# Value products of a head pair as one block, with the row sums, ahead of the third maxima, scores and projection

## The chip, the cores and the metric

The kernel runs on one core of a Trainium2 chip. The metric is the device time of one launch in microseconds. A core has five engines that run at the same time, each with its own instruction stream in a fixed order: TensorE (PE, matrix products; its weight loads are shown apart as PEld), VectorE (DVE), ScalarE (ACT), GpSimd (POOL) and SyncE (SP, which issues transfers). They wait for one another with semaphores only. Matrix products are written to PSUM, eight banks of 128 partitions by 512 floats; operands lie in SBUF.

## What the kernel computes

Two gated layers on tokens `x` (4 batches of 256 tokens, 128 channels) with a context `ctx` (4 batches of 512). The change is in the attention of the second layer: the tokens are latents that ask, context and latents together (768 keys) are the keys and values, 16 heads of 64 channels:

```
q = lat @ Wq
kv = concat([x, lat], axis=1) @ Wkv
k, v = split(kv)
dots = einsum('bhid,bhjd->bhij', q, k) * scale
attn = softmax(dots, axis=-1)
out = einsum('bhij,bhjd->bhid', attn, v)
return out.reshape(b, m, heads * dim_head) @ Wout
```

Around it, in order: an attention with 16 heads of 8 channels, a feed-forward layer with routed low-rank experts, this attention, and a feed-forward layer with one expert of eight per token. Every step adds its gated output to `x`.

## The kernel before, in words

The whole kernel is written by hand as one stream of instructions per engine, with the semaphore waits written out; no planner moves anything. The order in the Python text of an engine's block is the order in which that engine runs.

The second attention works on head pairs: 4 batches of 8 pairs, 32 pairs `g`, with `p = g % 8` the pair's place in its batch. One turn of the loop at L2235 (called turn `g` here) mixes the work of several pairs on TensorE:

- `max1(g+1, 0)`, `max1(g+1, 1)`, `max1(g+1, 2)` (L2027): the scores of the next pair, laid with queries on the partitions, only to find their row maxima. All three write banks 4 and 5, so each waits until VectorE has reduced the one before (`row_max1`, L1337: reductions at L1343 for parts 0 and 1 and at L1346 for part 2, then a small maximum at L1352 that makes `max_cols`).
- `max_row_in(g+1)` (L2050): turns those maxima into a row. It waits for L1352. ScalarE copies the row out, and `scores1(g+1, 0)` waits for that copy.
- `scores1(g, 0)`, `(g, 1)`, `(g, 2)` (L2056): the scores of pair `g` with keys on the partitions, less the maxima. ScalarE takes the exponential of each third (`exp1`, L813).
- `project(g+3, 0)` and `project(g+3, 1)` (L1993): keys and queries of a pair three ahead, into bank 7. ScalarE copies each half out rounded (`kqh`, L572), VectorE subtracts to get the rest (`proj_low`, L1331, `kql`, L1334), and that frees bank 7.
- `values1(g-1, chunks)` (L2079): values times probabilities of the pair before, six chunks of 128 keys, into the left half of bank 6. `sums1(g-1)` (L2097): the row sums, into the right half of bank 6, from `fold1`, which GpSimd has folded from the probabilities (two additions, L551 and L554, and a fold, L559).
- at the end of a turn `values_in` (into bank 5) and a third use of bank 7: a value projection, the turned context or latents of the next batch (`context_turn`, `latents_turn`, for `p` = 3 and 4), or the output projection of the batch before (`outputs1`, for `p` = 1). The third use waits until bank 7 is free, that is for `kql` of `project(g+3, 1)`.

VectorE runs a turn in this order (L1557 to L1583):

```
row_max1(g + 1, 0)
...
row_max1(g + 1, 1)
proj_low(g + 3, 0)
...
first_slot(g)
row_max1(g + 1, 2)
second_slot(g)
proj_low(g + 3, 1)
...
divide1(g - 1)
```

`divide1` (L1355: a reciprocal at L1359 and a product at L1360) waits for `sums1` and reads bank 6. The slots hold the normalising of the next batch's tokens for `p` = 3 (`context_norm`, L1296, in the first, `latents_norm`, L1285, in the second), steps of the layer norm for some other turns, and for `p` = 4 and 5 a copy `kv_t` (L1306, L1322) stands between `row_max1(g + 1, 0)` and `row_max1(g + 1, 1)`.

Of the kernel before, what the change touches and what calls it, by code (L numbers as in the profile page):

```python
# [47 lines left out]
def flamingo(nc, t_in, out):  # L48
# [24 lines left out]
    G1 = B * NPAIR  # L73
# [4 lines left out]
    with ExitStack() as ctx:  # L78
# [152 lines left out]
        def bank(i, n=1):  # L231
            return ps[:, i * BANK:(i + n) * BANK]
# [146 lines left out]
        def values_of(b, half):  # L379

            m = max(M_AT[u] for u in M_USES if u[:2] == (b, half)) + 1
            x = max(VX_AT[u] for u in VX_AT if u[1:3] == (b, half)) + 1
            return m, x
# [1241 lines left out]
        def _(pe):  # L1625
            def mm(o, lhsT, rhs, start=True, stop=True):
                return pe.matmul(o, lhsT, rhs, start=start, stop=stop)  # L1627
# [399 lines left out]
            def max1(g, part):  # L2027
                s = g % KS
                if part == 0:
                    pe.wait_ge(d_kql.sem, d_kql.after(g, 2))  # L2030
                    if g >= 1:
                        pe.wait_ge(d_max1.sem, d_max1.after(g - 1, 4))
                        pe.wait_ge(a_mrow.sem, g)
                    m = sum(1 for use in M_USES if M_PAIR[use] <= g - 2)
                    if m:
                        pe.wait_ge(a_vM.sem, m)
                else:
                    pe.wait_ge(d_max1.sem, d_max1.after(g, part))
                q = kqh[:, s, NK:NK + NQ]
                if part < 2:  # L2040
                    for j in range(2):
                        ins = mm(bank(4 + j), q[half_of[j], part * P:(part + 1) * P], kqh[half_of[j], s, 0:NC_])
                else:
                    for t in range(TQ):
                        for j in range(2):
                            ins = mm(bank(4 + j)[:, t * NQ:(t + 1) * NQ], q[half_of[j], t * P:(t + 1) * P],
                                     kqh[half_of[j], s, NC_:NK])
                ins.then_inc(e_max1.sem, 1)

            def max_row_in(g):  # L2050
                pe.wait_ge(d_max1.sem, d_max1.after(g, 4))
                for t in range(TQ):
                    ins = mm(tok(bank(4), t), max_cols[:, g % 2, t, :], negidentb[:, :])
                ins.then_inc(e_mrow.sem, 1)

            def scores1(g, u):  # L2056
                n = 3 * g + u
                s = g % KS
                if u == 0:
                    pe.wait_ge(a_mrow.sem, g + 1)  # L2060
                if n == 1:
                    pe.wait_ge(d_kql.sem, d_kql.after(2, 2))
                if n >= 2:
                    pe.wait_ge(a_exp1.sem, n - 1)
                q_h, q_l = kqh[:, s, NK:NK + NQ], kql[:, s, NK:NK + NQ]
                for k in (2 * u, 2 * u + 1):
                    o = [bank(2 * (n % 2) + j)[:, (k % 2) * NQ:(k % 2 + 1) * NQ] for j in range(2)]
                    at = slice(k * P, (k + 1) * P)
                    for j in range(2):
                        mm(o[j], kqh[half_of[j], s, at], q_h[half_of[j], :], True, False)  # L2070
                    for j in range(2):
                        mm(o[j], kql[half_of[j], s, at], q_h[half_of[j], :], False, False)
                    for j in range(2):
                        mm(o[j], kqh[half_of[j], s, at], q_l[half_of[j], :], False, False)
                    for j in range(2):
                        ins = mm(o[j], onesb[half_of[j], :], max_row[half_of[j], g % 2, :], False, True)
                ins.then_inc(e_st1.sem, 1)

            def values1(g, chunks):  # L2079
                b, p = divmod(g, NPAIR)  # L2080
                if chunks[0] == 0:
                    if g >= 1:
                        pe.wait_ge(d_o1.sem, g)
                    if p % 4 == 0:
                        m, x = values_of(b, p // 4)
                        pe.wait_ge(a_vM.sem, m)
                        pe.wait_ge(a_vX.sem, x)
                pe.wait_ge(a_exp1.sem, a_exp1.after(g, chunks[-1] // 2 + 1))
                for k in chunks:
                    for j in range(2):  # L2090
                        h = 2 * p + j
                        ins = mm(bank(6)[j * D1:(j + 1) * D1, 0:NQ], v1[:, k, h * D1:(h + 1) * D1],
                                 p1[:, g % 2, k // 2, j * BANK + (k % 2) * NQ:j * BANK + (k % 2 + 1) * NQ],
                                 k == 0, k == TK - 1)
                ins.then_inc(e_pv1.sem, 1)

            def sums1(g):  # L2097
                pe.wait_ge(g_fold.sem, g + 1)
                for j in range(2):
                    ins = mm(bank(6)[j * D1:(j + 1) * D1, NQ:2 * NQ], onesf[:, :], fold1[:, g % 2, j, :])  # L2100
                ins.then_inc(e_den1.sem, 1)
# [55 lines left out]
            def turned_in1(i):  # L2157
                pe.wait_ge(d_xnD.sem, i + 1)
                if i == 0:
                    pe.wait_ge(d_kql.sem, d_kql.after(G1, 0))  # L2160
                if i == 1:
                    pe.wait_ge(d_o1.sem, G1)
                if i >= 2:
                    pe.wait_ge(a_mT.sem, i)
                transpose_tiles(bank(HEAD_BANK[i]), xnD[:, i % 2, :, :], TQ).then_inc(e_xTD.sem, 1)

            def head1(i):
                pe.wait_ge(a_xTD.sem, i + 1)
                mm(bank(HEAD_BANK[i])[0:E, NQ:2 * NQ], gate1[:, :], xTD[:, i % 2, :]).then_inc(e_lgD.sem, 1)

            def probs1(i):
                pe.wait_ge(d_prob.sem, i + 1)
                if i >= 1:
                    pe.wait_ge(a_b2.sem, i)
                transpose_tiles(bank(7), probT[:, :].rearrange("p (t d) -> p t d", t=TQ), TQ).then_inc(e_pT.sem, 1)

            def masks1(i):
                pe.wait_ge(d_mask.sem, i + 1)
                transpose_tiles(bank(HEAD_BANK[i]), maskp[:, i % 2, :, :], TQ).then_inc(e_mT.sem, 1)
# [55 lines left out]
            for g in range(G1 + 1):  # L2235
                b, p = divmod(g, NPAIR)
                if g < G1:
                    if g + 1 < G1:
                        max1(g + 1, 0)
                    scores1(g, 0)  # L2240
                    if g == G1 - 3:
                        turned_in1(0)
                    if g == G1 - 2:
                        probs1(0)
                    scores1(g, 1)
                    if g + 1 < G1:
                        max1(g + 1, 1)
                    if g + 3 < G1:
                        project(g + 3, 0)
                    if g == G1 - 3:  # L2250
                        head1(0)
                    if g == G1 - 1:
                        masks1(0)
                        wide_masks1(0, 0)
                if g == G1:
                    wide_masks1(0, 1)
                    bias1(0)
                if g >= 1:
                    values1(g - 1, (0, 1, 2, 3))
                if g < G1:  # L2260
                    if g + 1 < G1:
                        max1(g + 1, 2)
                    scores1(g, 2)
                    if g + 3 < G1:
                        project(g + 3, 1)
                if g >= 1:
                    values1(g - 1, (4, 5))
                    sums1(g - 1)
                if g < G1:
                    if g + 1 < G1:  # L2270
                        max_row_in(g + 1)
                    if values_use(g) is not None:
                        values_in(*values_use(g))
                    use = third_use(g)
                    if use is not None:
                        if use[0] == "v":
                            values_in(*use[1:])
                        elif use[0] == "ctx":
                            context_turn(use[1])
                        elif use[0] == "lat":  # L2280
                            latents_turn(use[1])
                        else:
                            outputs1(use[1])
# [52 lines left out]
```

## Time and profile before

| what | us |
|---|---|
| median of 3 runs | 828.2 (823.18 to 828.38) |
| the profiled execution | 827.83 |
| its span, first to last instruction | 826.0 |
| PE busy | 740.4 (90%) |
| DVE busy | 574.0 (69%) |
| ACT busy | 360.6 (44%) |
| POOL busy | 282.4 (34%) |

The profiled execution takes 1.8 us more than its span, and 0.4 us less than the median. A row of a timeline gives the start and the duration of an instruction (or of several of one kind that follow each other, with their count), its engine, line, operation, output and inputs, and in brackets how long the engine stood idle before it and whose instruction ended that. TensorE runs each product of 32-bit floats in two passes, so the count of its rows is twice the number of products in the text.

### The profile page before, as it was taken

How to read it: one execution, taken by the hardware profiler on the slowest of the kernel's cores; microseconds unless marked ns; L12 is line 12 of the kernel's file. 1: busy time of each engine (PE TensorE's matmuls, PEld its weight loads, DVE VectorE, ACT ScalarE, POOL GpSimd, SP SyncE). 2: the span in 40 equal slices, each digit the busy share in tenths (PEclk: the TensorE clock that was granted, in tenths of full speed). 3: DMA queues.
4: the chain of work that ended last, by engine and by line, in shares of the span. 5: the costliest groups of instructions: out<-in, count | busy, mean ns of one | idle time of the engine just before them, and what ended most of it. 6: DMA issues, size and time to landing. Idle time of an engine off the chain costs nothing.

```text
span 826.0 us, 14271 instructions
## 1 busy us (share of the span) xinstructions
PE 740.4 (90%) x5654; PEld 549.9 (67%) x5654; DVE 574.0 (69%) x1100; ACT 360.6 (44%) x533; POOL 282.4 (34%) x203
## 2 busy tenths in 40 slices
PE   6779989996987997889999899989999787999996
PEld 5656556654776875656777677766677555887894
DVE  4767777654778686897667876587767876577543
ACT  2666665762343435345444445444444333320300
POOL 4265444410100102454554455445554453100000
PEclk9789999997999998999999999999999998999998
DMA  8000000005000021000000000000000000000000
GB/s 175 9 1 2 2 1 2 2 2 204 2 1 0 1 70 34 1 1 2 1 2 1 2 1 2 1 1 2 1 2 2 1 1 1 1 8 1 7 7 6
DMA packets 25552, 11.55 MB, mean 14 GB/s; under 512 B 11832, under 2 KB 24200, under 8 KB 25360
## 3 DMA queue, kind: packets, MB, share of 16 engines
q1 hardware_dynamic: 24480, 10.59, 5.0%
q8 instruction: 45, 0.74, 0.4%
q10 hardware_dynamic: 1008, 0.07, 0.1%
q14 instruction: 19, 0.16, 0.1%
HBM read 10.06 MB, written 0.52 MB: 13 GB/s over the span
## 4 chain that ended last, share of the span: by engine, by line
PE 71%; DVE 20%; issue 4%; ACT 3%; DMA 1%; SPq 0%; DVEq 0%; ACTq 0%
PE ps L1627 68%; PE ps L1638 2%; DVE mx L1068 2%; DVE o L1359 2%; ACT v L572 1%; DVE max_cols L1352 1%; DVE pmax L1343 1%; DVE pmax L1346 1%; DVE xnC L1285 1%; DVE kql L1334 1%; DVE ysum L1494 1%; DVE cn L1296 1%; ACT kqh L572 1%; PE ps L1731 1%; DMA raw<-in_L_xattn_Wproj_dram 1%
## 5 line engine op out<-in xcount | busy, mean ns | idle before, releaser
L813 ACT ACTIVATE p<-ps 128x1024 f32<-128x1024 f32 x96 | 96.7, 1025 | 146.1 <-PE ps L1627 146.1
L1627 PE MATMUL ps<-p,v 128*64 128x256 f32 (+1 forms) x1280 | 131.9, 389 | 4.1 <-DVE xr L1091 2.0
L551 POOL TENSOR_TENSOR acc<-p 128x1024 f32<-128x1024 f32 x32 | 76.0, 2374 | 154.7 <-ACT p L813 154.7
L1627 PE MATMUL ps<-kqh 64*128 64x256 f32 (+1 forms) x640 | 109.9, 379 | 11.9 <-ACT v L572 4.3
L1068 DVE TENSOR_REDUCE mx<-ps 128x1 bf16<-128x512 f32 x128 | 82.5, 687 | 34.7 <-PE ps L1627 33.9
L1343 DVE TENSOR_REDUCE pmax<-ps 128x2 f32<-128x1024 f32 x64 | 78.2, 1222 | 38.4 <-PE ps L1627 37.2
L554 POOL TENSOR_TENSOR acc<-acc,p 128x1024 f32<-128x1024 f32 x32 | 76.0, 2375 | 69.7 <-ACT p L813 69.7
L1627 PEld LDWEIGHTS ps<-p,v 128*64 128x64 f32 (+1 forms) x1280 | 64.0, 126 | 53.1 <-issue 18.9
L1627 PEld LDWEIGHTS ps<-kqh 64*128 64x128 f32 x640 | 62.0, 202 | 37.6 <-issue 29.5
L524 POOL TENSOR_SCALAR q<-qst,rmask 128x256 fp32r<-128x256 f32 x64 | 58.9, 938 | 65.3 <-ACT qst L572 65.3
L668 ACT ACTIVATE p<-ps 128x1024 f32<-128x1024 f32 x64 | 65.4, 1025 | 27.8 <-PE ps L1627 25.8
L1334 DVE TENSOR_TENSOR kql<-ps,kqh 128x512 fp32r<-128x512 f32 x64 | 44.1, 691 | 34.2 <-ACT kqh L572 33.9
L1359 DVE RECIPROCAL o<-ps 128x256 f32<-128x256 f32 x32 | 56.2, 1755 | 6.2 <-PE ps L1627 3.6
L1627 PE MATMUL ps<-max_row,onesb 64*128 64x256 bf16 x384 | 59.8, 293 | 0.0
L1627 PE MATMUL ps<-kqh,kql 64*128 64x256 f32 x384 | 59.5, 292 | 0.0
L1627 PE MATMUL ps<-kql,kqh 64*128 64x256 f32 x384 | 58.8, 288 | 0.0
L1627 PE MATMUL ps<-kst,q 128*128 128x512 f32 x128 | 49.1, 435 | 4.6 <-DVE mx L1068 4.2
L1346 DVE TENSOR_REDUCE pmax<-ps 128x4 f32<-128x1024 f32 x32 | 39.1, 1220 | 18.9 <-PE ps L1627 18.8
L1627 PE MATMUL ps<-q,kst 128*128 128x256 f32 x256 | 46.7, 304 | 0.4 <-ACT p L668 0.4
L1627 PEld LDWEIGHTS ps<-q,kst 128*128 128x128 f32 x256 | 34.5, 189 | 13.5 <-issue 7.0
L572 ACT ACTIVATE kqh<-ps 128x512 fp32r<-128x512 f32 x64 | 38.0, 594 | 11.0 <-PE ps L1627 8.5
L1627 PEld LDWEIGHTS ps<-kqh,kql 64*128 64x128 f32 x384 | 41.9, 201 | 0.5
(282 smaller groups left out, 1561.8 us busy)
## 6 DMA issues: line engine op xcount, KB each, us to landing
w<-in_L_ffn_W_dram SPq DMA_DIRECT2D x1, 2048.0 KB, 12.0
wt<-in_L_ffn_W_dram SPq DMA_DIRECT2D x4, 512.0 KB, 6.1
ctx_all<-in_ctx_dram SPq DMA_DIRECT2D x4, 256.0 KB, 5.4
raw_kv<-in_L_xattn_Wkv_dram SPq DMA_DIRECT2D x1, 1024.0 KB, 4.9
raw<-in_L_ffn_B_dram SPq DMA_DIRECT2D x9, 64.0 KB
xr<-in_x_dram SPq DMA_DIRECT2D x4, 128.0 KB, 3.9
raw_q<-in_L_xattn_Wq_dram SPq DMA_DIRECT2D x1, 512.0 KB, 5.8
wout<-in_L_xattn_Wout_dram SPq DMA_DIRECT2D x1, 512.0 KB, 7.1
```

Source lines behind the costliest of these rows:

```text
L524: pool.tensor_scalar(q4[:, q % SLOTS, v, :], qst[:, q % 2, :], rmask[:, v:v + 1], None, ALU.mult).then_inc(g_q4.sem, 1)
L551: pool.tensor_tensor(acc1[:, :], p1[:, s, 0, :], p1[:, s, 1, :], ALU.add).then_inc(g_acc.sem, 1)
L554: pool.tensor_tensor(acc1[:, :], acc1[:, :], p1[:, s, 2, :], ALU.add).then_inc(g_acc.sem, 1)
L572: return act.activation(to, of, ACT.Copy)
L668: act.activation(p0[:, n % PR0, :], bank(2 * (n % 2), 2), ACT.Exp).then_inc(a_exp0.sem, 1)
L813: act.activation(p1[:, g % 2, u, :], bank(2 * (n % 2), 2), ACT.Exp, scale=SCALE1).then_inc(a_exp1.sem, 1)
L1068: dve.tensor_reduce(mx0[:, q % 2, n % 2, n // 2:n // 2 + 1], bank(4 + m % 2), AX, ALU.max).then_inc(d_max0.sem, 1)
L1334: dve.tensor_tensor(kql[:, g % KS, at], bank(X_BANK.get(("proj", g, half), 7)), kqh[:, g % KS, at], ALU.subtract).then_inc(d_kql.sem, 1)
L1343: dve.tensor_reduce(pmax[:, g % 2, 0, part, :], m.rearrange("p (j k) -> p j k", j=2), AX, ALU.max).then_inc(d_max1.sem, 1)
L1346: dve.tensor_reduce(pmax[:, g % 2, 1, :, :].rearrange("p t j -> p j t"), m.rearrange("p (j t k) -> p j t k", j=2, t=TQ), AX, ALU.max).then ...
L1359: then(dve.reciprocal(o1[:, g % OS, :], bank(6)[:, NQ:2 * NQ]))
L1627: return pe.matmul(o, lhsT, rhs, start=start, stop=stop)
```

## The change

In the loop over pairs on TensorE the second part of the value products and the row sums move up: they come straight behind the first four chunks, ahead of `max1(g+1, 2)`, `scores1(g, 2)` and `project(g+3, 1)`. No instruction is added or removed, no wait changes, and the streams of the other engines stay as they are.

```
                 if g >= 1:
                     values1(g - 1, (0, 1, 2, 3))
+                    values1(g - 1, (4, 5))
+                    sums1(g - 1)
                 if g < G1:
                     if g + 1 < G1:
                         max1(g + 1, 2)
                     scores1(g, 2)
                     if g + 3 < G1:
                         project(g + 3, 1)
-                if g >= 1:
-                    values1(g - 1, (4, 5))
-                    sums1(g - 1)
-                if g < G1:
                     if g + 1 < G1:
                         max_row_in(g + 1)
```

## Rows read from the trace of the kernel before

**Rows 1.** The page: busy time by engine, and the chain of waits by engine.
```profile
PE 740.4 (90%) x5654; PEld 549.9 (67%) x5654; DVE 574.0 (69%) x1100; ACT 360.6 (44%) x533; POOL 282.4 (34%) x203
...
PE 71%; DVE 20%; issue 4%; ACT 3%; DMA 1%; SPq 0%; DVEq 0%; ACTq 0%
```

**Rows 2.** Timeline of PE, turn 17: start us, duration us, what.
```profile
516.62 0.50 PE L1627 MATMUL ps<-kqh 64*128 64x512 f32 x2
...
519.83 0.63 PE L1627 MATMUL ps<-kqh 64*128 64x256 f32 x6
...
522.13 1.08 PE L1627 MATMUL ps<-p,v 128*64 128x256 f32 x8
...
523.58 0.28 PE L1627 MATMUL ps<-negidentb,max_cols 128*128 128x128 bf16 x2
...
524.44 3.73 PE L1627 MATMUL ps<-wout,o 128*128 128x128 f32 x32
...
530.28 0.48 PE L1627 MATMUL ps<-kqh 64*128 64x512 f32 x2
```

**Rows 3.** Timeline of DVE, turns 13, 14, 16 and 17.
```profile
473.85 1.23 DVE L1343 TENSOR_REDUCE pmax<-ps 128x2 f32<-128x1024 f32 x1 [0.47 <-PE ps L1627]
...
484.81 1.23 DVE L1343 TENSOR_REDUCE pmax<-ps 128x2 f32<-128x1024 f32 x1 [0.92 <-PE ps L1627]
...
506.71 1.23 DVE L1343 TENSOR_REDUCE pmax<-ps 128x2 f32<-128x1024 f32 x1 [0.92 <-PE ps L1627]
...
515.36 1.21 DVE L1343 TENSOR_REDUCE pmax<-ps 128x2 f32<-128x1024 f32 x1
517.17 1.23 DVE L1343 TENSOR_REDUCE pmax<-ps 128x2 f32<-128x1024 f32 x1 [0.60 <-PE ps L1627]
...
521.63 0.18 DVE L1352 TENSOR_TENSOR max_cols<-pmax 128x4 bf16<-128x4 f32 x1
522.87 0.69 DVE L1334 TENSOR_TENSOR kql<-ps,kqh 128x512 fp32r<-128x512 f32 x1 [1.06 <-ACT kqh L572]
```

**Rows 4.** Timeline of DVE, turns 3 and 5 (one row each), 11 and 12.
```profile
355.75 1.23 DVE L1343 TENSOR_REDUCE pmax<-ps 128x2 f32<-128x1024 f32 x1 [0.93 <-PE ps L1627]
...
380.45 1.22 DVE L1343 TENSOR_REDUCE pmax<-ps 128x2 f32<-128x1024 f32 x1 [0.47 <-PE ps L1627]
...
448.36 1.22 DVE L1343 TENSOR_REDUCE pmax<-ps 128x2 f32<-128x1024 f32 x1 [0.92 <-PE ps L1627]
...
452.37 1.21 DVE L1346 TENSOR_REDUCE pmax<-ps 128x4 f32<-128x1024 f32 x1
...
453.69 3.74 DVE L1285 TENSOR_SCALAR xnC<-xr,token_moments,rt_y 128x128 f32<-128x128 f32 x2
457.36 0.68 DVE L1334 TENSOR_TENSOR kql<-ps,kqh 128x512 fp32r<-128x512 f32 x1
457.96 1.74 DVE L1359 RECIPROCAL o<-ps 128x256 f32<-128x256 f32 x1
...
460.08 1.21 DVE L1343 TENSOR_REDUCE pmax<-ps 128x2 f32<-128x1024 f32 x1
461.21 0.80 DVE L1306 TENSOR_SCALAR kv_t<-ps,lncols 128x512 f32<-128x512 f32 x1
```

**Rows 5.** Timeline of POOL: the second addition in turns 11 and 28.
```profile
453.63 2.38 POOL L554 TENSOR_TENSOR acc<-acc,p 128x1024 f32<-128x1024 f32 x1 [2.03 <-ACT p L813]
...
656.42 2.37 POOL L554 TENSOR_TENSOR acc<-acc,p 128x1024 f32<-128x1024 f32 x1 [5.77 <-ACT p L813]
```

**Rows 6.** Timeline of DVE: normalising in turn 28, a divide in turn 31.
```profile
655.66 0.60 DVE L1285 TENSOR_SCALAR xnD<-xr,token_moments,rt_y 128x128 f32<-128x128 f32 x2
...
692.59 1.76 DVE L1359 RECIPROCAL o<-ps 128x256 f32<-128x256 f32 x1 [3.57 <-PE ps L1627]
```

**Rows 7.** Timeline of PE: the turned context at the end of turn 11.
```profile
458.09 0.66 PE L1638 MATMUL ps<-ident,cn 128*128 128x128 f32 x4 [2.30 <-DVE kql L1334]
```

**Rows 8.** Stretch behind that wait: busy us of each engine, then TensorE's granted clock.
```profile
458.10:462.50 4.40, 4.40 (x40) 3.47 (x40) 3.87 (x4) 1.31 (x2) 0.00 (x0) 0.68 0.02 6
```

More of the change, by code:

```diff
@@ L2259, in _ @@
                     values1(g - 1, (0, 1, 2, 3))
+                    values1(g - 1, (4, 5))
+                    sums1(g - 1)
                 if g < G1:
@@ L2265, in _ @@
                         project(g + 3, 1)
[L2266 to L2269, printed above, removed]
                     if g + 1 < G1:
```

## The prediction, on record before the run

> **What bounds the kernel now.** I read the page first: TensorE is busy 90% of the span and holds 71% of the chain of waits, VectorE 20% [rows 1]. So most of the time is TensorE's, and a change of its order pays only where it stands idle. Then I took the timelines of the second attention, engine by engine, for turns of every kind, because shares over the span don't tell what a turn waits for.
>
> A plain turn (one from `max1(g+1,1)` to the next) lasts 10.96 us: the reductions of that part start at 473.85 and 484.81 [rows 3]. TensorE fills it nearly whole. But VectorE is close behind: in turn 17 the reduction of `max1(g+1,0)` runs from 515.36, with no idle time before it, since the divide before it has only just ended, and `max1(g+1,1)` starts on TensorE at 516.62, right when that reduction is done [rows 2, 3]. That is the point to watch: VectorE's queue has the divide between the last `kql` of a turn and the first reduction of the next, and TensorE can't go past `max1(g+1,1)` without that reduction.
>
> Turns with `p` = 3 are different. There the reduction of part 2 comes late, at 452.37, behind the normalising of the context; the two `latents_norm` operations then take 3.74 us, while GpSimd's second addition runs from 453.63 for 2.38 us; `kql` waits behind them until 457.36 and the context's turn on TensorE stands idle 2.30 us for it [rows 4, 5, 7]. Behind that gap the mean granted clock is 0.68 for 4.4 us [rows 8], a mixture of 2.4 and 1.2 GHz.
>
> **The change part by part.** Nothing is added, removed or made to wait anew; no DMA and no instruction of SP, ACT, DVE or POOL moves in its own queue. What moves on TensorE is four products and two row sums: from 522.13 to the next instruction at 523.58, 1.45 us [rows 2].
>
> *Inputs of the moved block.* The probabilities and the fold of pair g-1 are done in turn g-1, and `divide1(g-2)`, which frees bank 6, ends before `max1(g+1,1)`. I cost waits of the block itself at nothing; what covers it is a whole turn.
>
> *What stands behind the block now.* Part 2 of the maxima, the last third of scores and `project(g+3,1)` come 1.45 us later. The row of maxima has its `max_cols` ready 1.98 us behind the start of part 2 (519.83 to 521.63 plus 0.18), and the scores and projection take 2.30 us (519.83 to 522.13) [rows 2, 3]: it still costs nothing, but the slack falls from 1.8 us to 0.3.
>
> *The loop through VectorE.* This is the main cost. The divide no longer waits for the sums but for its place in the queue, behind `kql` of the later projection. Round the loop, for a plain turn: `max1(g+1,1)` to part 2 took 3.21 us (516.62 to 519.83), now with the block 4.66; to the projection's end 2.30; ScalarE's copy until `kql` starts 0.74 (522.13 to 522.87); `kql` to the reciprocal 0.60 (457.36 to 457.96, the turn in which nothing stood between them); reciprocal and product until the next reduction 2.12 (457.96 to 460.08); that reduction until `max1(g+1,1)` of the next turn 1.26 (515.36 to 516.62) [rows 2 to 4]. The sum is 11.68 us, above TensorE's 10.96. So a plain turn grows by 0.72.
>
> Would VectorE take the divide early, since its sums are there? In turn 31 it stood idle 3.57 us in front of a reciprocal [rows 6], although a subtraction for the last layer's weights (L1547), whose input ScalarE had long made, stood further back in its queue. So it doesn't pass a waiting instruction, and I charge the loop in full. The Trainium skill, "TensorE: Matmul & The Clock Gate", section "Architectural detail: the array is 16× 32×32, not 1× 128×128", says the same against this change: VectorE's queue is strictly first in, first out. By that rule the sum is about 838; an engine that took whichever was ready would give about 820, as in the first rival.
>
> By kinds of turn:
> - 13 plain turns (`p` = 2 four times; 5, 6 and 7 three times each): 13 x 0.72 = +9.4.
> - `p` = 0, three turns: they last 10.46 (506.71 to 517.17 [rows 3]), as only one use of the banks ends them. They too become 11.68: 3 x 1.22 = +3.7.
> - `p` = 1 with the output projection, three turns: 13.66 now (516.62 to 530.28). Bank 7 comes free only when `kql` ends, 0.74 + 0.69 behind the projection, and 0.05 later the next product starts (458.04 to 458.09) [rows 3, 4, 7]; from the output projection on it takes 5.84 (524.44 to 530.28 [rows 2]). 4.66 + 2.30 + 1.48 + 5.84 = 14.28: 3 x 0.62 = +1.9.
> - `p` = 3 with the turn behind it, three pairs: 24.70 once (355.75 to 380.45) and 25.49 in the other two (448.36 to 473.85) [rows 3, 4]. Here the delay helps. In turn 11 the reduction of part 2 started with no idle time in front of it: VectorE came straight from normalising the context, and 1.26 us later the addition began (452.37 to 453.63). Now the scores come 1.45 us later and the addition, which follows their exponential, with them, while the context's normalising stays where it is; the queue runs dry and the reduction starts on time. Turn 28 shows what is then left: both normalising operations took 0.60 us, to 656.26, and the addition began at 656.42 [rows 4 to 6]. I take it that they get through. Then the pair costs 2 x 11.68, plus 0.2 because `kv_t` ends 0.67 us behind `max1(g+1,1)` (461.21 + 0.80 against 460.08 + 1.26 [rows 4]) and holds the next projection: 23.56. Change: -1.14 and twice -1.93, -5.0.
> - Turns 1 and 27 have steps of a layer norm in the slots; between nothing and 0.7 each, half taken: +0.8. Turns 28 to 30: TensorE or the last gating chain holds them; nothing taken, 0.7 each as the upper end and as much below.
> - Turn 31: the divide that waited 3.57 us [rows 6] gets its sums ahead of a third of scores, about half of the 2.30: -1.1, which reaches the end, since the last pair waits for that divide.
>
> For how the normalising meets GpSimd the Trainium skill, "SBUF — State Buffer", section "Who interferes with whom", says that the two share a port pair and whoever issues first holds it for its whole instruction. Rows 4 to 6 agree (3.74 us against 0.60), and by that rule a margin of 0.16 us decides the -5.0.
>
> Sum: 9.4 + 3.7 + 1.9 - 5.0 + 0.8 - 1.1 = +9.7. The profiled execution took 827.83, so 837.5; the median of the runs is 0.4 higher, and I predict **838 us**. Ends: 0.15 us of error in the loop over 22 turns is 3, turns 1 and 27 to 30 give 3 either way; with them 832 to 844.
>
> **The rivals.**
>
> *VectorE's loop doesn't bind (not slower).* Place: the divide in front of the first reduction. If the loop is under 10.96, that is if my pieces of 11.68 overlap by 0.72 us more than in the rows they come from, plain turns and `p` = 0 stay as they are, and the turns at `p` = 3 and 4 shrink to 2 x 11: -2.7 and twice -3.5. With +1.9, +0.8 and -1.1 that is -8.1: **820**. For it: the sum is made of rows from different turns, and a change of tile shapes less on TensorE may save a little. Against: every piece is an order in a queue, and turn 17 shows the loop closing already.
>
> *The normalising doesn't get through.* If GpSimd's addition still comes first, each of the three pairs only shifts by 1.45: +4.4 instead of -5.0, **847**. For it: the margin of 0.16 us. Against: turn 28.
>
> *The clock falls.* In turns `p` = 0 and 1 TensorE now stands idle up to 1.4 us in front of the third use of bank 7. The gap of 2.30 us was followed by a clock of 0.68 over 4.4 us [rows 7, 8], which costs 4.4 x 0.32 = 1.4 us. In all six turns it would be +8: **846**; if plain turns fell too, more. Against: those six gaps are shorter than that one.
>
> That the change doesn't do what it says is no rival: TensorE runs the text's order.
>
> **How the numbers follow.** My forecast 0.60, VectorE's loop not binding 0.12, normalising blocked 0.16, clock 0.12. About 1% (8.3 us) is what a measurement of this kernel can tell from no change, so slower begins at 836.5, in the upper two thirds of the forecast's own range: 0.41, with the two slow rivals 0.69. The first rival lies on the lower bound, 819.9: 0.07 faster and 0.05 within; with 0.19 of the forecast the middle has 0.24. The range takes in the forecast, the two slow rivals and the upper part of what lies between forecast and first rival: 829 to 849.
>
> **What would show it.** Right: in plain turns the reciprocal starts at the end of `kql` with no idle time, the reductions of `max1(g+1,1)` follow each other by about 11.7 us, and TensorE waits at `max1(g+1,1)` for a reduction; at `p` = 3 the two `xnC` take 0.6 us and the wait of the turned context falls to about 0.5. Wrong: turns of 10.96 (first rival), `xnC` of several us (second), or rows of 1.2 GHz behind the third use (third).

## The result, and the profile after

The changed kernel takes 843.05 us (median of four runs, 836.16 to 845.33) against 828.29 for the kernel before (four runs, 823.18 to 829.79): a ratio of 1.0175, 95% interval 1.010 to 1.025. It is slower, as forecast, and inside the range; the forecast was 5 us short. The profiled execution took 841.65 us, its span is 839.8, 13.8 more than before.

The page of the kernel after, busy time by engine and the chain by engine, answers to [rows 1]:

```profile
PE 739.4 (88%) x5654; PEld 545.3 (65%) x5654; DVE 559.7 (67%) x1100; ACT 357.3 (43%) x533; POOL 283.9 (34%) x203
...
PE 68%; DVE 20%; issue 7%; ACT 4%; DMA 1%; SPq 0%; ACTq 0%; DVEq 0%
```

TensorE does the same work in the same busy time and fills less of a longer span: it is not busy for 100.4 us (839.8 less 739.4), where it was 85.6. So the question is where TensorE waits. The waits of TensorE in the kernel after, from 315 to 712 us (total, number of times, longest):

```profile
PE ps L1627 <- DVE kql L1334: 13.4, 20, 1.3
PE ps L1627 <- DVE pmax L1343: 8.5, 10, 2.8
PE ps L1627 <- DVE maskb L1434: 4.6, 1, 4.6
...
PE ps L1627 <- POOL fold L559: 1.8, 1, 1.8
```

The first line was one wait of 0.7 us before; it now comes 20 times. The last two are single waits at the end of the attention and did not exist before.

**A plain turn.** Timeline of DVE in the kernel after, turn 14, against [rows 3]:

```profile
485.10 1.22 DVE L1343 TENSOR_REDUCE pmax<-ps 128x2 f32<-128x1024 f32 x1 [0.60 <-PE ps L1627]
...
492.11 0.69 DVE L1334 TENSOR_TENSOR kql<-ps,kqh 128x512 fp32r<-128x512 f32 x1 [1.06 <-ACT kqh L572]
492.71 1.75 DVE L1359 RECIPROCAL o<-ps 128x256 f32<-128x256 f32 x1
494.50 0.42 DVE L1360 TENSOR_TENSOR o<-ps,o 128x256 f32<-128x256 f32 x1
494.84 1.21 DVE L1343 TENSOR_REDUCE pmax<-ps 128x2 f32<-128x1024 f32 x1
496.64 1.23 DVE L1343 TENSOR_REDUCE pmax<-ps 128x2 f32<-128x1024 f32 x1 [0.59 <-PE ps L1627]
```

And of PE in the same turn, against [rows 2]:

```profile
484.55 0.50 PE L1627 MATMUL ps<-kqh 64*128 64x512 f32 x2
...
485.89 2.81 PE L1627 MATMUL ps<-p,v 128*64 128x256 f32 x24
488.53 0.60 PE L1627 MATMUL ps<-fold,onesf 128*64 128x256 f32 x4
489.06 0.62 PE L1627 MATMUL ps<-kqh 64*128 64x256 f32 x6
...
491.25 0.28 PE L1627 MATMUL ps<-negidentb,max_cols 128*128 128x128 bf16 x2
...
492.85 0.50 PE L1627 MATMUL ps<-wkv_h,kv_h 128*128 128x512 f32 x1 [0.56 <-DVE kql L1334]
...
495.87 0.28 PE L1627 MATMUL ps<-max_row,onesb 64*128 64x256 bf16 x2
496.11 0.49 PE L1627 MATMUL ps<-kqh 64*128 64x512 f32 x2
```

The end of the same scores and the start of `max1(g+1,1)` in the kernel before, one turn earlier:

```profile
484.23 0.30 PE L1627 MATMUL ps<-max_row,onesb 64*128 64x256 bf16 x2
484.27 0.50 PE L1627 MATMUL ps<-kqh 64*128 64x512 f32 x2
```

Read the two together. The sums of the divide start at 488.53, yet the reciprocal starts only at 492.71, straight behind `kql`: its place in the queue holds it, not its data. Four VectorE operations then run without a gap, and `max1(15,1)` starts on TensorE at 496.11, right behind the reduction (494.84 plus 1.21). TensorE waits about 0.20 us for it, which no bracket shows: 0.24 us lie between the start of the last products of the scores and that of `max1`, where 0.04 lay before. The longer wait of the turn, 0.56 us, is the one for `kql` in front of the third use of bank 7. The turn is 11.54 us (485.10 to 496.64), where it was 10.96.

**The turn with `p` = 3.** DVE of the kernel after, turn 11, against [rows 4]:

```profile
454.63 1.22 DVE L1346 TENSOR_REDUCE pmax<-ps 128x4 f32<-128x1024 f32 x1 [0.63 <-PE ps L1627]
...
455.97 0.60 DVE L1285 TENSOR_SCALAR xnC<-xr,token_moments,rt_y 128x128 f32<-128x128 f32 x2
457.13 0.69 DVE L1334 TENSOR_TENSOR kql<-ps,kqh 128x512 fp32r<-128x512 f32 x1 [0.57 <-ACT kqh L572]
```

The reduction now waits for its scores, the two `xnC` take 0.60 us instead of 3.74, and GpSimd's second addition of this turn begins at 456.69, just behind their end at 456.57.

**By kinds of turn** (us from one reduction of `max1(g+1,1)` to the next):

| turns | before | after | change of one | forecast |
|---|---|---|---|---|
| plain | 10.95 | 11.55 | +0.60 | +0.72 |
| `p` = 0 | 10.46 | 11.55 | +1.09 | +1.22 |
| `p` = 1 | 13.63 | 14.20 | +0.57 | +0.62 |
| `p` = 3 and 4, three pairs | 24.70, 25.49, 25.50 | 23.38, 23.38, 23.37 | -1.32, -2.11, -2.13 | -1.14, -1.93, -1.93 |

From turn 1 to turn 30 the sum is +8.8 us (330.48 to 674.68 before, 328.06 to 681.05 after; forecast +10.8). Ahead of turn 1 the execution after is 2.4 shorter, in code that the change does not touch. The rest (called the tail here), from the reduction in turn 30 to the end, went from 151.32 to 158.75 us: +7.4, where I had -1.1. That is the surprise.

**The end of the attention.** Stretches of the kernel after: from turn 30's reduction to the turned mask products, to the last layer's first products, through the first 16 of these, to the end (busy us of PE, PEld, DVE, ACT, POOL, then the granted clock):

```profile
681.05:696.55 15.50, 9.77 (x84) 6.19 (x85) 12.02 (x20) 4.50 (x6) 9.13 (x4) 0.83 0.01 2
696.55:712.42 15.87, 11.30 (x95) 7.33 (x95) 11.19 (x8) 3.30 (x4) 4.50 (x2) 0.82 0.00 1
712.42:717.95 5.53, 5.53 (x18) 4.51 (x18) 0.00 (x0) 3.64 (x5) 0.00 (x0) 0.62 0.00 0
717.95:839.80 121.85, 110.10 (x675) 95.33 (x673) 69.47 (x130) 21.39 (x37) 6.40 (x4) 0.97 0.02 5
```

The same four of the kernel before:

```profile
674.68:686.69 12.01, 9.41 (x85) 6.71 (x85) 10.60 (x20) 4.35 (x6) 5.99 (x3) 0.78 0.01 1
686.69:700.76 14.07, 10.39 (x96) 6.87 (x94) 8.94 (x8) 4.34 (x6) 5.99 (x3) 0.94 0.01 2
700.76:704.21 3.45, 3.45 (x18) 3.04 (x17) 0.00 (x0) 3.22 (x5) 0.00 (x0) 1.00 0.00 0
704.21:826.00 121.79, 110.03 (x675) 95.33 (x673) 69.42 (x130) 21.81 (x38) 6.41 (x4) 0.98 0.02 5
```

The loss lies in the first three: 3.5 + 1.8 + 2.1 us. `w_l` (L1547) is the subtraction for the last layer's weights, `maskb` (L1434) the masks by which that layer picks its expert. DVE of the kernel after there:

```profile
690.55 2.06 DVE L1547 TENSOR_TENSOR w_l<-wt,w_h 128x1024 fp32r<-128x1024 f32 x1
692.53 3.96 DVE L1434 TENSOR_SCALAR maskb<-iota_ed,topf 128x1024 bf16<-128x1024 bf16 x2
```

POOL of the kernel after:

```profile
689.14 2.39 POOL L554 TENSOR_TENSOR acc<-acc,p 128x1024 f32<-128x1024 f32 x1 [5.81 <-ACT p L813]
691.60 2.13 POOL L559 TENSOR_TENSOR fold<-acc 128x512 f32<-128x512 f32 x1
693.87 2.34 POOL L551 TENSOR_TENSOR acc<-p 128x1024 f32<-128x1024 f32 x1
```

And PE of the kernel after:

```profile
680.93 5.23 PE L1627 MATMUL ps<-p,v 128*64 128x256 f32 x24
...
696.55 1.03 PE L1627 MATMUL ps<-identb,maskb 128*128 128x128 bf16 x8 [4.62 <-DVE maskb L1434]
...
708.66 0.65 PE L1627 MATMUL ps<-fold,onesf 128*64 128x256 f32 x4 [1.80 <-POOL fold L559]
...
712.42 5.69 PE L1627 MATMUL ps<-xm,w 128*128 128x256 f32 x16
```

In the kernel before the same two operations stood at another moment, with GpSimd idle (its fold ended at 682.78, its next addition began at 687.42):

```profile
683.50 1.21 DVE L1547 TENSOR_TENSOR w_l<-wt,w_h 128x1024 fp32r<-128x1024 f32 x1
684.63 0.87 DVE L1434 TENSOR_SCALAR maskb<-iota_ed,topf 128x1024 bf16<-128x1024 bf16 x2
```

After the change the subtraction `w_l` meets the addition (2.06 us instead of 1.21), the fold meets `w_l` (2.13 instead of about 1.28), and the masks meet the fold and the next addition (3.96 instead of 0.87). TensorE waits 4.62 us for the masks. The kernel before had another collision here: `max_cols` of turn 30 met the addition and took 2.02 us, and TensorE waited 2.13 for it. In the kernel after, the block of values of turn 30 (24 rows for twelve products; the rounded products of scores and projections have one row each) takes 5.23 us, for which turn 14 needed 2.81: nearly twice as long, at a granted clock of 0.53, so mostly at the lower of the two clock levels (1.2 GHz of 2.4). The last layer's first 16 products take 5.69 instead of 3.62, at a granted clock of 0.62.

### The profile page after: what moved, and what is told of

It is laid out like the page before. It is cut to its first block, busy times and chain, and to the rows that moved or that the text cites. A ratio compares the mean times of both kernels' runs of the same rounds, so it can differ in the third digit from the quotient of the medians.

```text
span 839.8 us, 14271 instructions
## 1 busy us (share of the span) xinstructions
PE 739.4 (88%) x5654; PEld 545.3 (65%) x5654; DVE 559.7 (67%) x1100; ACT 357.3 (43%) x533; POOL 283.9 (34%) x203
## 2 busy tenths in 40 slices
DMA packets 25552, 11.55 MB, mean 14 GB/s; under 512 B 11832, under 2 KB 24200, under 8 KB 25360
## 4 chain that ended last, share of the span: by engine, by line
PE 68%; DVE 20%; issue 7%; ACT 4%; DMA 1%; SPq 0%; ACTq 0%; DVEq 0%
PE ps L1627 66%; DVE o L1359 2%; ACT kqh L572 2%; DVE kql L1334 2%; DVE mx L1068 2%; PE ps L1638 2%; DVE pmax L1343 1%; DVE w_l L1547 1%; DVE ysum L1494 1%; DVE pmax L1346 1%; DVE rt_t L1262 1%; PE ps L1731 1%; DMA raw<-in_L_xattn_Wproj_dram 1%; DVE rs_t L945 1%; DVE maskb L1434 0%
## 5 line engine op out<-in xcount | busy, mean ns | idle before, releaser
L1627 PE MATMUL ps<-p,v 128*64 128x256 f32 (+1 forms) x1280 | 128.7, 393 | 2.9 <-DVE xr L1091 2.0
L1627 PE MATMUL ps<-kqh 64*128 64x256 f32 (+1 forms) x640 | 104.8, 370 | 13.7 <-DVE pmax L1343 9.1
L1627 PEld LDWEIGHTS ps<-p,v 128*64 128x64 f32 (+1 forms) x1280 | 68.4, 130 | 55.0 <-issue 22.7
L1627 PEld LDWEIGHTS ps<-kqh 64*128 64x128 f32 x640 | 56.2, 192 | 41.0 <-issue 23.4
L1627 PE MATMUL ps<-max_row,onesb 64*128 64x256 bf16 x384 | 55.5, 282 | 0.0
L1627 PE MATMUL ps<-kqh,kql 64*128 64x256 f32 x384 | 55.3, 281 | 0.0
L1627 PE MATMUL ps<-kql,kqh 64*128 64x256 f32 x384 | 54.6, 278 | 0.0
L559 POOL TENSOR_TENSOR fold<-acc 128x512 f32<-128x512 f32 x32 | 42.8, 1336 | 2.5
```

## Experiments

**Theory.** The loss in the turns is the loop through VectorE's queue: `kql`, divide, first reduction, `max1(g+1,1)`, block, part 2, projection, `kql`. What counts is how much work stands between `max1(g+1,1)` and the projection.

**Rivals:** another wait (bank 7, the clock, the block as such) sets the longer turn; GpSimd's additions, met at other moments, are the whole loss. The kernel before, run again beside them, took 825.58 us beside the first four and 823.98 beside the last four; ratios are against these.

**Only the values move.** The row sums stay behind the projection (the edit against the changed kernel):

```
                     values1(g - 1, (4, 5))
-                    sums1(g - 1)
                 ...
                         project(g + 3, 1)
+                if g >= 1:
+                    sums1(g - 1)
```

> Only the two last chunks of the value products move up; the row sums stay in front of the row of maxima. Theory (the loop through VectorE: what is put in front of the later projection delays kql, the divide behind it, the first reduction and so the next max1 part 1): a plain turn falls from the 11.55 us of the changed kernel by the length of the row sums, 0.53 us, to about 11.0. Rival (the block as such costs, by its changes of tile shape on TensorE): a plain turn stays at 11.5 or more, as there is one change of shape more. Device time by the theory: some 12 us under the changed kernel, 827 to 833; by the rival 840 or more.

Measured: 828.01 us, ratio 1.0022 (0.9988 to 1.0056), plain turns 11.11, `p` = 1 turns 13.77, the two `xnC` 0.60 together. In a plain turn of this kernel the trace shows no wait of TensorE for bank 7, the reciprocal still starts straight behind `kql`, and `max1` waits about 0.15 us for its reduction: here it is the loop through the divide that holds the turn. The values are 0.92 of the 1.45 us that the change puts in front of part 2, and cost 0.16 us a turn; the sums, the other 0.53 us, cost a further 0.44. That is what a loop does that had some slack first: 0.76 of the 0.92 us went into it, hardly any of the 0.53.

**The block at `p` = 3 alone.** The new order in turns 3, 11 and 19, the old one elsewhere:

```
+                early = p == 3 and b + 1 < B
                 ...
+                if g >= 1 and early:
+                    values1(g - 1, (4, 5))
+                    sums1(g - 1)
                 ...
-                if g >= 1:
+                if g >= 1 and not early:
                     values1(g - 1, (4, 5))
                     sums1(g - 1)
```

> The new order only in the three turns p = 3 of batches 0 to 2, the old one in all others. Theory: the gain there (the two xnC get through before GpSimd's addition) needs no other turn, and the loss of the plain turns is gone: xnC 0.60 us in place of 3.74 in all three, three pairs of turns shorter by 1.5 to 2.5 us each, plain turns 10.95; 6 us faster than the kernel before, 820 to 824. Rival (the gain at p = 3 comes from the whole loop being slower, so that VectorE has time to spare): xnC still 3.7 us, time as before, 827 to 830.

Measured: 821.77 us, ratio 0.9955 (0.9931 to 0.9978); plain turns 10.95, `p` = 3 turns 11.59 and the turn behind them 11.2, the two `xnC` 0.60. So the change's good part is real and lies in these three turns. The tail of this execution, where nothing differs from the kernel before, took 153.55 us, not 151.32, with a wait of 4.2 us for the masks: the collisions of the tail are not the new order's alone.

**The old order in the last four turns.** The new one for `g` < 28, otherwise the edit of the version above:

```
+                early = g < G1 - 4
```

> The new order in turns 0 to 27, the old one in 28 to 31. Theory: 7 us of the loss arise in the tail, where maskb and w_l of VectorE now run against GpSimd's fold and addition (maskb 3.96 us in place of 0.87, its masks' product waits 4.6 us, and the last layer starts behind the gap at a low clock). With the old order there maskb takes 0.9 us and the time falls by 5 to 7 us against the changed kernel, to 835 to 838. Rival (the tail only inherits a shifted phase from the earlier turns): maskb stays at 2 us or more, time 840 to 844.

Measured: 835.31 us, ratio 1.0105 (1.0067 to 1.0143), the time as expected. The mechanism I gave missed: the masks were blocked here too. DVE of this kernel:

```profile
688.57 2.32 DVE L1547 TENSOR_TENSOR w_l<-wt,w_h 128x1024 fp32r<-128x1024 f32 x1
690.82 2.95 DVE L1434 TENSOR_SCALAR maskb<-iota_ed,topf 128x1024 bf16<-128x1024 bf16 x2
```

From turn 30's reduction to the end it took 153.6 us, against 158.75 with the new order. So the order in the last four turns costs about 5 us against this execution; the remaining 2 of the 7.4 lie between two executions of the old order. Little of the 5 is a longer wait for the masks (4.20 us here, 4.62 there). Its three stretches are 1.9, 1.2 and 2.1 us shorter than those of the kernel after, with granted clocks of 0.88, 0.90 and 1.00 in place of 0.83, 0.82 and 0.62.

**The divide made cheap.** The changed kernel with a copy in place of reciprocal and product:

```
-                then(dve.reciprocal(o1[:, g % OS, :], bank(6)[:, NQ:2 * NQ]))
-                dve.tensor_tensor(o1[:, g % OS, :], bank(6)[:, 0:NQ], o1[:, g % OS, :],
-                                  ALU.mult).then_inc(d_o1.sem, 1)
+                dve.tensor_copy(o1[:, g % OS, :], bank(6)[:, 0:NQ]).then_inc(d_o1.sem, 1)
```

> The changed kernel with the divide left out: instead of reciprocal and product VectorE only copies the value products (about 0.4 us in place of 2.2), so the outputs are not divided by the row sums. Theory: the loop through VectorE falls under 10 us, but bank 7 still comes free only with the later kql, so the third use keeps its 0.5 us of waiting and a plain turn falls only to about 11.45. Rival (the divide is the whole cost): a plain turn falls to the 10.95 of before.

Measured once: 814.18 us, plain turns 11.34, where 11.45 was expected. VectorE now idles in front of the first reduction, and TensorE still waits for bank 7. DVE of this kernel (its lines are two lower from the divide on):

```profile
480.65 0.69 DVE L1334 TENSOR_TENSOR kql<-ps,kqh 128x512 fp32r<-128x512 f32 x1 [1.06 <-ACT kqh L572]
481.26 0.41 DVE L1359 COPY o<-ps 128x256 f32<-128x256 f32 x1
482.83 1.22 DVE L1343 TENSOR_REDUCE pmax<-ps 128x2 f32<-128x1024 f32 x1 [1.16 <-PE ps L1625]
```

And PE:

```profile
481.40 0.50 PE L1625 MATMUL ps<-wkv_h,kv_h 128*128 128x512 f32 x1 [0.54 <-DVE kql L1334]
```

So the divide sets the turn, but only 0.2 us above a second bound: with values and sums gone from behind the projection, too little is left on TensorE to cover `kqh` and `kql` before bank 7 is used again. Without the divide a turn is still 0.39 longer than before, so the shift of work ahead of the projection costs on both paths, and the wait for bank 7 alone would give most of the 0.60. The tail of this kernel, in the new order, took 151.33 us although its masks were held up too (4.00 us): TensorE waited only 2.02 us for them.

**GpSimd's second addition cut, old order, and cut, new order.** In both kernels the addition works on 32 of 1024 columns:

```
-pool.tensor_tensor(acc1[:, :], acc1[:, :], p1[:, s, 2, :], ALU.add).then_inc(g_acc.sem, 1)
+pool.tensor_tensor(acc1[:, 0:32], acc1[:, 0:32], p1[:, s, 2, 0:32], ALU.add).then_inc(g_acc.sem, 1)
```

> The kernel before with GpSimd's second addition (L554) cut to 32 of 1024 columns, so that the row sums lack most of the last third of the keys; all waits stay. Theory: xnC was slow because that addition held the port that VectorE needs, so xnC takes 0.6 us in the old order too, the turned context no longer waits 2.3 us, and the blocked max_cols of turns 0, 1, 27 and 30 (2.1 us) take 0.18; the time falls by 8 to 14 us, to 812 to 818. Rival (xnC is slow by itself or by the late reduction): xnC stays at 3.7 us, time within 3 us of before.

> The same cut in the changed kernel (row sums lack most of the last third). Theory: the gain at p = 3 is then in both kernels and only the loop through VectorE is left of the change: plain turns 11.55 against 10.95; 0.6 us in 13 plain turns and three pairs, 1.1 in three turns p = 0, 0.6 in three turns p = 1, some 17 us in all over the kernel before with the same cut; 829 to 836. The tail's maskb falls to 0.9 us. Rival (the loss is contention with GpSimd as well): the two kernels with the cut are within 5 us.

Measured: old order 805.75 us, ratio 0.9773 (0.9737 to 0.9809), new order 821.40, ratio 0.9955 (0.9926 to 0.9984). The cut by itself gained more than I expected of it, 18 us, so the absolute time of the second missed too; its distance to the first, 15.65 us, is near the 17 expected. What was blocked before is seen in the groups of `max_cols` (shortest, median, longest in ns). The kernel before:

```profile
L1352 DVE TENSOR_TENSOR max_cols<-pmax x32: 175/177/2082, 312.0 to 679.4; 128x4 bf16<-128x4 f32 x32
```

Old order with the addition cut:

```profile
L1352 DVE TENSOR_TENSOR max_cols<-pmax x32: 175/177/180, 310.4 to 659.8; 128x4 bf16<-128x4 f32 x32
```

One expectation missed here: the two `xnC` of the old order took 1.63 us, not 0.60, because GpSimd's fold, now early, runs over them (445.50 to 446.77 against 445.22 to 446.86 in turn 11).

With the addition cut, the new order still makes plain turns of 11.55 and turns 1 to 30 last 348.25 us, 18.5 more than the old (329.74): the loop needs no contention. And the tail is 146.9 in the new order against 147.5 in the old. This sum hides three parts. Up to the last layer's first products the new order is 0.6 us shorter (9.21 + 12.43 against 8.91 + 13.31), where it was 5.3 longer with the addition: that part of the loss needs the addition, and the masks take 0.87 us in both. The first 16 products take 1.7 us longer with the new order here too, so their low clock does not need it. The PE row of the new order with the addition cut, at a granted clock of 0.69 (3.62 us for these products in the old, at 1.00), behind a wait of 2.84 us (2.41 in the old):

```profile
697.80 5.31 PE L1627 MATMUL ps<-xm,w 128*128 128x256 f32 x16
```

The rest of the last layer was 1.7 us shorter in that execution, in code that the change does not touch; its last 43 us had a granted clock of 0.99, where the old order's last 45 had 0.92.

**All six chunks and the sums behind the projection.** A block too, but on the other side:

```
-                if g >= 1:
-                    values1(g - 1, (0, 1, 2, 3))
                 ...
                         project(g + 3, 1)
                 if g >= 1:
+                    values1(g - 1, (0, 1, 2, 3))
                     values1(g - 1, (4, 5))
                     sums1(g - 1)
```

> All six chunks and the sums as one block, but behind maxima part 2, the last scores and the later projection instead of ahead of them. Theory (place, not block): kql is early, the divide waits for the sums and not the other way round; the loop through VectorE is about 10.7 us, and a plain turn is TensorE's own work plus about 0.5 us of waiting for the reduction of part 1 in front of part 2: 11.2 us; at p = 3 xnC is blocked again (3.7 us); 828 to 834 in all. Rival (one block costs wherever it stands): plain turns at 11.5 or more, over 838.

Measured: 826.99 us, ratio 1.0023 (0.9995 to 1.0051), a little below what I expected; plain turns 11.30. The 0.35 that they lose come from the wait that I had expected: part 2 now follows the first projection at once, and TensorE waits for the reduction of part 1 (the divide in turn waits for its sums). PE of this kernel:

```profile
505.83 0.62 PE L1627 MATMUL ps<-kqh 64*128 64x256 f32 x6 [0.42 <-DVE pmax L1343]
```

Part 2 comes early here, and `max_cols` meets the addition in the turns `p` = 3, 4 and 5 (1.08, 1.86 and 1.60 us; the turns last 12.32, 11.28 and 12.28). At `p` = 3 the two `xnC` behind it take 1.56 us, not the 3.7 expected: the addition is over by then, and only the fold runs against them. DVE of this kernel, `p` = 5:

```profile
473.11 1.21 DVE L1346 TENSOR_REDUCE pmax<-ps 128x4 f32<-128x1024 f32 x1
474.35 1.60 DVE L1352 TENSOR_TENSOR max_cols<-pmax 128x4 bf16<-128x4 f32 x1
```

So making one block is not what gives the 11.55; what it costs depends on what it is put in front of.

**The values early at `p` = 3, the sums never.** The two experiments on dose and place point to this version: the two chunks move up in the four turns with `p` = 3, everything else is the old order.

```
+                early = p == 3
                 ...
+                    if early:
+                        values1(g - 1, (4, 5))
                 ...
-                    values1(g - 1, (4, 5))
+                    if not early:
+                        values1(g - 1, (4, 5))
                     sums1(g - 1)
```

> Old order except in the four turns p = 3, where the last two chunks move up but the sums stay. Theory: xnC needs only the 0.9 us of the two chunks to get through, and the sums left behind shorten those turns by another 0.4 us each against the version that moves both: xnC 0.6 us, turns p = 3 of 11.1 us, 819 to 823. Rival (the sums' 0.5 us are needed as well): xnC 3.7 us, 825 to 829.

Measured: 815.05 us, ratio 0.9882 (0.9850 to 0.9913), better than expected and than both kernels. DVE of this kernel, turn 11:

```profile
451.43 0.18 DVE L1352 TENSOR_TENSOR max_cols<-pmax 128x4 bf16<-128x4 f32 x1
451.51 0.60 DVE L1285 TENSOR_SCALAR xnC<-xr,token_moments,rt_y 128x128 f32<-128x128 f32 x2
452.67 0.69 DVE L1334 TENSOR_TENSOR kql<-ps,kqh 128x512 fp32r<-128x512 f32 x1 [0.57 <-ACT kqh L572]
```

0.92 us of delay are enough for `xnC` to get ahead of the addition (452.11 against 452.23), and the sums behind the projection keep cover for bank 7: `p` = 3 turns 11.15, the turn behind them 11.2, plain turns 10.95. The fourth of these turns, 27, gained nothing (14.68, before 14.37).

## Why the prediction was right, and where it was not

*The loop through VectorE: right.* In turn 14 its pieces are 4.51 us to part 2, 2.19 to the projection's end, 0.86 to `kql`, 0.60, 2.13 and 1.27: 11.56 for the 11.68 forecast. The difference is in the first: the six chunks as one group hold TensorE for 2.64 us (485.89 to 488.53), where four and two apart took 1.87 and 0.92 before. That a change of tile shape falls away is my reading; no run tests it. The plain turns thus gave 0.60 instead of 0.72, and `p` = 0 and 1 followed. The rows for it: the reciprocal straight behind `kql`, and the dose in the first experiment. The rival by which the loop does not bind fell with the plain turns of 11.55, in the kernel after and again without the addition.

The Trainium skill, "TensorE: Matmul & The Clock Gate", section "Architectural detail: the array is 16× 32×32, not 1× 128×128", calls VectorE's queue strictly first in, first out. The trace agrees: the sums of turn 14 ended at 489.13 (488.53 plus 0.60), and the reciprocal that reads them started 3.58 us later, when the operations ahead of it in the queue were done.

*A bound that I did not name.* The divide holds the turn only 0.2 us above the third use of bank 7 (11.34 without it). I had written that gaps open there, as a risk to the clock, and not that they are the next limit. On TensorE's side the 0.60 of a plain turn are the 0.56 in front of the third use and the 0.20 in front of `max1(g+1,1)`, less the 0.15 saved in the block. The forecast's loop is the longer of the two paths, but by itself it decides a third of the growth.

*`p` = 3: right.* The scores came later, the normalising did not, and the two `xnC` got through, by 0.12 us where I had read a margin of 0.16. The pairs became 5.6 us shorter, for 5.0 forecast, and the turned context waits 0.55 us in place of 2.30. The rival by which they stay blocked fell with 0.60 us for the two.

*The clock in the turns: right to give it little.* TensorE waits 1.31 us in front of the third use in turn 16 (`p` = 0) and 0.56 in turn 17, and both turns have a granted clock of 1.00.

*Small turns: wrong in sign, small.* Turns 1 and 27 gave -0.4 and -0.6 for the +0.8 taken (half of twice 0.7 would have been 0.7); turn 2 gave 1.2 more than a plain turn, because the lower clock level behind a wait of 2.80 us in turn 1 fell on it (0.90 granted), and turn 29 took 1.2 more than before. Turn 2 was nearly as long with the old order in it (12.53 us where the block moved at `p` = 3 alone), so that part is not the change's.

*Turn 31: the term that failed, inside a sum that held.* By this term the divide gets its sums ahead of a third of scores, and -1.1 reaches the end. The sums did come earlier, and VectorE's idle time in front of that reciprocal fell from 3.57 us [rows 6] to 2.94. But I costed the last turns by the sums alone. `w_l` and the masks stand behind the divide on VectorE; I did not ask which moment they would move to, and it was the one at which GpSimd adds. The runs show +7.4 in the tail in place of -1.1. Four executions with the old order there and the whole addition lie between 150.6 and 153.6 us, so the new order's 158.75 costs 5 to 8; with the values alone moved up it was 156.0. With the addition cut the term has its forecast sign up to the last layer's first products, -0.6. What lowers the clock at these products, and how the rest divides into blocking and clock, stays open, and all these sizes come from single executions.

*The sum: in part luck.* The profiled executions differ by +13.8 where I had +9.7. The turns gave 2.0 less than forecast, the tail 8.5 more, and the 2.4 ahead of turn 1 have nothing to do with the change: these misses partly cancel.

## What to carry to other kernels

Work that moves on one engine moves everything behind it; follow what stands behind it into the queues of the other engines until the path closes on itself, and add up that loop: here TensorE had no more work, and a turn grew because the later projection left TensorE nothing to do while bank 7 was being freed (0.39 of the 0.60 remain without the divide), and because VectorE's fixed order put the divide into the way of the next turn. A reorder that helps in a few turns and costs in all others belongs into those few: the two chunks moved at `p` = 3 alone gave -1.2%, the whole change +1.75%. And where two engines block each other, list for every moved stretch, the tail too, which operations of the one come to lie under which of the other; shifts of about a microsecond decided here whether `xnC` took 0.60 or 3.74 us and the masks 0.87 or 3.96.

## What the runs showed of the hardware

Blocking between VectorE and GpSimd goes both ways: GpSimd's fold took 2.13 us instead of about 1.28 when `w_l` ran first. The Trainium skill, "SBUF — State Buffer", section "Who interferes with whom", says that a VectorE instruction with two inputs in SBUF contends with a GpSimd instruction that reads SBUF, and that whoever issues first gets the shared port pair for the whole instruction. The trace agrees to within 0.16 us: `w_l` started 0.98 us before the addition's end and took 0.85 longer, the fold started 1.01 us before `w_l`'s end and took 0.85 longer. A small operation is held up as well: a `max_cols` of four elements a partition, 0.18 us alone, took up to 2.08.

GpSimd's second addition, 2.4 us in each of 32 pairs, cost the kernel before 18 us of 824 (2.3%). No wait of TensorE for the fold behind it is in that trace; the turns that gained most without it are those in which VectorE's small operations had met it (turn 0 from 14.29 to 11.43 us, turn 1 from 14.38 to 12.46, the `p` = 3 turns from 13.57 or more to 11.46 or less).
